# A fused four-layer graph network on one core: the first weight quarter loaded ahead of the activations, the first scale in halves, the first weight product read by VectorE, and three quarters of the second product computed later

## The chip, the core and the metric

One program on one core of a Trainium2 chip. The metric is the device time of the program in microseconds (us), median of several runs; lower is better. The engines are TensorE (PE for matmuls, PEld for the loading of their stationary side), VectorE (DVE), ScalarE (ACT), GpSimd (POOL) and the queue of SyncE (SP, or SPq), which issues most of the DMAs.

## The reference, cut to what matters

Four layers over 128 graphs of 64 nodes with 512 features (8192 rows in all). Each layer starts with a layer norm without weights and a relu, and adds its result to x. The first two are the ones whose setup the change touches:

```python
# layer 0
h = relu(layernorm(x))
q, k = split(h @ Wqk); v = h @ Wv
w = mask * sum(q * (adj @ (k * mask))) / sqrt(512)      # one number per row
x = x + softmax(w, axis=1)[:, :, None] * v
# layer 1
h = relu(layernorm(x))
weight = adj * exp((h @ Wq.T + bq) @ (h @ Wk.T + bk).T)
x = x + (weight / weight.sum(2)) @ (h @ Wv.T + bv)
```

Layers 2 (eight-head attention) and 3 (three-hop diffusion) follow. The kernel never forms q and k in layers 0 and 1: it multiplies the two weight matrices once, M0 = Wq Wk^T of layer 0 (called m0) and A1 of layer 1 (called a1), and then needs h M0 h^T.

## The kernel before, in words

The 8192 rows are cut into 16 groups (NG) of 512, each of four tiles of 128 rows. Every engine has one program, written out by hand in the order in which it runs; semaphores tie them together. There is no scheduler. The groups run through layers 0 and 1 together: iteration g does layer 0 of group g and layer 1 of group g-1.

A product of full precision goes over the array in fp32r as three passes: hi by hi, hi by lo and lo by hi (`gemm_T`, L309, and `gemm`, L330; both of 48 matmuls a group and matrix). So each matrix is split into `hi` (a rounding copy, usually on ACT, `split_W` L977) and `lo` (source minus hi, on DVE, `split_W` L598, or on POOL).

The setup, in the order of each engine:

- SP issues (L1474 on): x of group 0 (1024 KB); four quarters k = 0..3 of layer 0's Wqk, each as a qT and a kTw part of 256 KB; three small loads (two biases in `bcol`, the node mask in `mcol`; semaphore d_b1 counts all three); wk1 (1024 KB). Then `gather(0, 0, (0, 1))` waits until DVE has made the four transposes of group 0 (v_tr) and issues 8 DMAs of 64 KB that finish the transposition of h (hs to hGA). Behind the gather stand wq1 (1024 KB), adj and mask of group 0, Wv of layer 0, Wv of layer 1 (1024 KB each), bv1, bqk, then x of group 1, adj of group 1, mask of group 1 and x of group 2.
- PE (L371 on): m0, 16 full fp32 matmuls in the order k outside, output quarter dc inside, so that all four PSUM banks are finished in the last round; `s0`, a small matmul; `rows1`, eight matmuls, four with wk1 and four with wq1; `product("a1", wk1, wq1, (0, 1))`, two of the four output quarters of a1 (4 fp32 matmuls each). Then iteration 0: `l01_g0` (g0 = M0 by h, four banks oc 0..3), tile 0 of `l01_v0`, the scores s0 (`scores`, L334), tiles 1..3 of v0, then the other two quarters of a1, crow and ucol. `l01_g0` waits for p_flo0 (lo of h) and for v_wlo (lo of m0). The scores wait for a_g0, that is, for ACT's copies of all four g0 banks.
- DVE (L703 on): statistics of x0 (`stats_A`), bsel and bprod from bcol (wait for d_b1), four transposes into hs, the four lo parts of m0, the lo parts of h (`features0_lo`), s0, the two rows, lo of a1's quarters 0 and 1; then in iteration 0 statistics of x1, and `transposes(0, 1)`.
- POOL: `scale_A(0, 0)` (L1236) turns the statistics of four tiles into scale and offset by four small instructions, once all four tiles' statistics are there; then the mask product and the lo part of Wv0.
- ACT (L1046 on): `norm_A(0, 0)` (four tiles), then 8 gather DMAs of its own (q = 2, 3), then the four hi copies of m0, the hi copies of h (`features2_hi`), hi of Wv0, hi of a1's quarters 0, 1. Iteration 0: copies of g0's banks 0 and 1, then `norm_A(0, 1)` (needs x1 and its statistics), then copies of g0's banks 2 and 3.

Two places carry much of what follows. On ACT the four norms of x1 stand between two pairs of g0's copies (three lines of the loop, put together here for g = 0):

```python
g0(g, (0, 1))      # L1057
norm_A(0, 1)       # L1067
g0(g, (2, 3))      # L1069
```

and on PE the scores need all four copies (L423). `hi_of` and `lo_dve` (L292, L293) are only the counts that the semaphores of hi and lo parts reach, in the order of the names.

Of the kernel before, what the change touches and what calls it, by code (L numbers as in the profile page):

```python
# [66 lines left out]
def rows(w):  # L67
    return w.rearrange("(c p) n -> p c n", p=128)
# [6 lines left out]
def build(nc, x, adj_rows, adj_cols, adj_heads, nodemask, L0_gnn_Wqk, L0_gnn_Wv, L1_gnn_Wq_w, L1_gnn_Wq_b, L1_gnn_Wk_w, L1_gnn_Wk_b,  # L75
# [11 lines left out]
    with root:  # L87
# [3 lines left out]
        def sems(names):  # L91
            return [sem(n) for n in names.split()]
# [24 lines left out]


        (c_pool, a_whi, v_wlo, p_wlo) = sems("consts_pool w_hi w_lo_dve w_lo_pool")
        (v_bsel, v_rows1, v_crow, v_ucol, p_one1) = sems("bias_cols rows1 crow ucol ones_v")  # L120
        (v_af, v_cst, p_bones, p_bsum) = sems("af cst bones bsum")

# [166 lines left out]

        hi_of = {n: 4 * i + 4 for i, n in enumerate(("m0", "v0", "a1", "v1", "q2", "k2", "v2", "o2", "w2", "w1", "w0"))}  # L292
        lo_dve = {n: 4 * i + 4 for i, n in enumerate(("m0", "a1", "v1", "q2", "k2", "v2", "o2"))}  # L293
        lo_pool = {n: 4 * i + 4 for i, n in enumerate(("v0", "w2", "w1", "w0"))}

# [1 line left out]
        def pe_program(eng):  # L297
# [85 lines left out]
            for j, (w, loaded, c0) in enumerate(((wk1, d_k1, 0), (wq1, d_q1, 4))):  # L383
# [3 lines left out]
                    ins = eng.matmul(b[32 * k:32 * k + 32, :], bsel[:, c0 + k, :], w[:, k, :], start=True, stop=True,  # L387
                                     tile_position=(0, 32 * k))
                ins.then_inc(full, 1)
            product("a1", wk1, wq1, (0, 1))  # L390

            def l01_g0(g, ocs):
                pe.wait_ge(p_flo0, 4 * g + 4)
# [18 lines left out]
            for g in range(NG + 1):  # L412
                on0, on1, on_pv = g < NG, g >= 1, g >= 2
                if on0:
                    l01_g0(g, (0, 1))
                if on_pv:
                    l01_pv(g - 2)
                if g == NG:
                    l2_gemm_T("q2", 0, Wq2, a_q)
                if on0:  # L420
                    l01_g0(g, (2, 3))
                    l01_v0(g, 0)
                    pe.wait_ge(a_g0, 4 * g + 4)  # L423
                    scores(("s0", g), gT[0], hGA, (v_am, g + 1))
                    for t in range(1, 4):
                        l01_v0(g, t)
                if on1:
                    pe.wait_ge(p_flo1, 4 * g)
                    pe.wait_ge(v_wlo, lo_dve["a1"])
                    for oc in range(4):  # L430
                        gemm_T(("g1", g - 1, oc), Wa1, hT[1], oc, (a_g1, 4 * (g - 1) + oc + 1))
                    l01_v1(g - 1, 0)
                    pe.wait_ge(a_g1, 4 * g)
                    scores(("s1", g - 1), gT[1], hGB, (a_ex, 4 * g))
                    for t in range(1, 4):
                        l01_v1(g - 1, t)
                else:
                    product("a1", wk1, wq1, (2, 3))
                    b, full, before = bank.take(("crow",), (v_crow, 1))
                    pe.wait_ge(*before)  # L440
                    pe.wait_ge(v_rows1, 3)
                    eng.matmul(b[:], ones1[:], crow1[:], start=True, stop=True).then_inc(full, 1)
                    b, full, before = bank.take(("ucol",), (v_ucol, 1))
                    pe.wait_ge(*before)
                    for d in range(4):
                        ins = eng.matmul(b[:, d:d + 1], urow[:, d * 128:(d + 1) * 128], ones1[:, 0:1], start=True, stop=True)
                    ins.then_inc(full, 1)
# [118 lines left out]
            for g in range(NG):  # L566
                i = g % 2
# [24 lines left out]
        def dve_program(eng):  # L592
# [113 lines left out]
            eng.tensor_copy(bsel[:, :, 0], bcol[:]).then_inc(v_bsel, 1)  # L706
            eng.tensor_tensor(bprod[:], bcol[:, 0:4], bcol[:, 4:8], ALU.mult).then_inc(v_bsel, 1)
            transposes(0, 0)
            split_W(Wm0, "m0")
            features0_lo()  # L710
            dve.wait_ge(*bank.done(("s0",)))
            eng.tensor_reduce(s0, bank.of(("s0",))[:, 0:4], AX, ALU.add).then_inc(v_rows1, 1)
            for j, row in enumerate((crow1, urow)):
                dve.wait_ge(*bank.done(("rows1", j)))
                eng.tensor_copy(row[:], bank.of(("rows1", j))[:]).then_inc(v_rows1, 1)
            split_W(Wa1, "a1", (0, 1))

            for g in range(NG + 1):
                on0, on1, on_pv = g < NG, g >= 1, g >= 2
                if on_pv:  # L720
                    l01_x2(g - 2)
                if g + 1 < NG:
                    stats_A(0, g + 1)
                    if g == 0:
                        transposes(0, 1)
                elif on0:
                    stats_A(2, 0)
                if on0:
                    dve.wait_ge(*bank.done(("s0", g)))
                    dve.wait_ge(p_am, g + 1)  # L730
                    eng.tensor_tensor(am[:], t4(bank.of(("s0", g))[:, 0:256]), am[:], ALU.mult).then_inc(v_am, 1)
                    dve.wait_ge(v_am, g + 1)
                    dve.wait_ge(c_pool, 6)
                    eng.tensor_reduce(wS, am[:], AX, ALU.add).then_inc(v_amr, 1)
                    dve.wait_ge(v_amr, g + 1)
                    dve.wait_ge(d_b1, 48)
                    eng.scalar_tensor_tensor(wS, wS, ISQ, mcol[:, 4 * g:4 * g + 4], ALU.mult, ALU.mult).then_inc(v_ws, 1)
                    l01_p(g)
                    if g >= 2:
                        transposes(*((0, g + 1) if g + 1 < NG else (2, 0)))  # L740
                    xt = xs[x_slot(kA(0, g))]
                    for t in range(4):
                        dve.wait_ge(*bank.done(("v0", g, t)))
                        dve.wait_ge(v_pcol, g + 1)
                        eng.scalar_tensor_tensor(xt[:, t, :], bank.of(("v0", g, t))[:], pcol[:, t:t + 1], xt[:, t, :],
                                                 ALU.mult, ALU.add).then_inc(v_x1, 1)
                        dve.wait_ge(v_x1, 4 * g + t + 1)
                        stats(stB, v_stB, a_nB, 4 * g + t, xt, t)
                    if g == 1:
                        transposes(0, 2)  # L750
                    if g == 0:
                        split_W(Wa1, "a1", (2, 3))
                        split_in_place(Wv1, "v1")
                    transposes(1, g)
                    if on1:
                        l01_dots(g)
                    if g == NG - 1:
                        split_in_place(Wq2, "q2")
                        features2_lo(0)
                else:  # L760
                    stats_A(2, 1)
                    transposes(2, 1)
                    split_in_place(Wk2, "k2")
                if on1:
                    for t in range(4):
                        dve.wait_ge(*bank.done(("v1", g - 1, t)))
                        dve.wait_ge(d_bv1, 16)
                        if g >= 2:
                            dve.wait_ge(*bank.done(("pvy", g - 2, 1)))
                        b3, bias3 = (v[:].rearrange("p (c n) -> p c n", c=2) for v in (bank.of(("v1", g - 1, t)), bv1))  # L770
                        eng.tensor_tensor(vf[:, t, :, 0:256], b3, bias3, ALU.add).then_inc(v_vf, 1)
                else:
                    dve.wait_ge(*bank.done(("crow",)))
                    eng.tensor_copy(crow[:], bank.of(("crow",))[:]).then_inc(v_crow, 1)
                    dve.wait_ge(*bank.done(("ucol",)))
                    eng.tensor_copy(ucol, bank.of(("ucol",))[:, 0:4]).then_inc(v_ucol, 1)
                    l01_dots(0)
# [193 lines left out]
        def act_program(eng):  # L971
# [71 lines left out]
                    act.wait_ge(*bank.done((n, g, m)))  # L1043
                    eng.activation(dst[:, m, :], bank.of((n, g, m))[:], ACT.Identity, bias=bqk[:, c0 + m:c0 + m + 1]).then_inc(done, 1)  # L1044

            norm_A(0, 0)  # L1046
            act.wait_ge(v_tr, 4)
            blocks(eng, hGA, (2, 3))
            split_W(Wm0, "m0")
            features2_hi(0, 0, hT[0])  # L1050
            split_in_place(Wv0, d_v0)
            split_W(Wa1, "a1", (0, 1))

            for g in range(NG + 1):
                on0, on1 = g < NG, g >= 1
# [12 lines left out]
                if on0:  # L1068
# [15 lines left out]
                    else:  # L1084
                        features2_hi(2, 0, hT2[0])
                    if g == 0:
                        split_W(Wa1, "a1", (2, 3))
                        split_in_place(Wv1, d_v1)
                        norm_B(0, range(4))
                if on1:  # L1090
# [127 lines left out]
        def pool_program(eng):  # L1218
# [17 lines left out]
            def scale_A(layer, g):  # L1236
                scale(stA, v_stA, p_stA, 4 * kA(layer, g) + 4, 0, 4)
# [21 lines left out]
            eng.memset(wz[:], 0.0).then_inc(c_pool, 1)  # L1259
            eng.memset(stB[:, :, 11], 0.0).then_inc(c_pool, 1)  # L1260
            pool.wait_ge(s_pool, mh)
            scale_A(0, 0)
            l01_am(0)
            split_in_place(Wv0, "v0")
            for g in range(NG + 1):
# [105 lines left out]
        def sp_program(eng):  # L1371
# [99 lines left out]


            qk_rows = rows(L0_gnn_Wqk)
            load_x(0, x_v[0])  # L1474
            for k in range(4):
                eng.dma_start(qT[:, k, :], qk_rows[:, k, :]).then_inc(d_qk[k], 16)
                eng.dma_start(kTw[:, k, :], qk_rows[:, 4 + k, :]).then_inc(d_qk[k], 16)
            eng.dma_start(bcol[:, 0:4], L1_gnn_Wq_b).then_inc(d_b1, 16)
            eng.dma_start(bcol[:, 4:8], L1_gnn_Wk_b).then_inc(d_b1, 16)
            eng.dma_start(mcol[:], nodemask_cols).then_inc(d_b1, 16)  # L1480
            eng.dma_start(wk1[:], rows(L1_gnn_Wk_w)).then_inc(d_k1, 16)
            gather(0, 0, (0, 1))
            eng.dma_start(wq1[:], rows(L1_gnn_Wq_w)).then_inc(d_q1, 16)
            load_adj(0)
            load_mask(0)
            eng.dma_start(Wv0["raw"][:], rows(L0_gnn_Wv)).then_inc(d_v0, 16)
# [175 lines left out]
```

## Time and profile before

| | |
|---|---|
| median of 3 runs | 2223.53 us (2223.47 to 2223.89) |
| the profiled execution: its own time | 2223.11 us |
| its span (first to last instruction) | 2221.3 us |
| PE busy | 2203.8 us (99%) |
| PEld / DVE / ACT / POOL busy | 1759.2 / 1356.5 / 776.6 / 740.4 us |
| share of PE in the chain that ended last | 97% |
| granted TensorE clock over the span | 1.000 |
| DMA over the span | 99 GB/s |

Busy times overlap, since the engines run side by side; a busy PE isn't PE at its peak. The chain that ended last is followed back from the last instruction to what released each step. What the change touches lies in the first 70 us of the span, so the 40 slices of the page (55 us each) say little about it and the trace is read there in order of time.

### The profile page before, as it was taken

The page shows a single profiled execution, that of the slowest core. Times are in us where ns is not written, and L with a number is a line of the kernel's source. Part 1 is how long each engine was busy: PE and PEld are TensorE (multiplying, and loading weights), DVE is VectorE, ACT ScalarE, POOL GpSimd, SP SyncE. Part 2 cuts the span into 40 slices and gives each one's busy share as a digit, 9 for nine tenths or more (in the row PEclk, how much of TensorE's full clock was granted, in tenths as well). Part 3 has the DMA queues.
Part 4 walks back from the last instruction along what each step waited for, and adds up shares of the span by engine and source line. Part 5 has one row for each costly group of instructions (what it writes and reads, how often), then busy time and mean ns, then how long its engine had stood idle before and what let it go on. Part 6 is the DMA issues. An engine that isn't in the chain of part 4 may idle for free.

```text
span 2221.3 us, 39182 instructions
## 1 busy us (share of the span) xinstructions
PE 2203.8 (99%) x15756; PEld 1759.2 (79%) x15756; DVE 1356.5 (61%) x2712; ACT 776.6 (35%) x1393; POOL 740.4 (33%) x926
## 2 busy tenths in 40 slices
PE   8999999999999999999999999999999999999999
PEld 5788888888888888888888888888877777777776
DVE  4575666666665676555655454555687575757542
ACT  3433333233323333333322333232444343434342
POOL 1443433343433423332322332332343131313130
PEclk9999999999999999999999999999999999999999
DMA  6333332333333344433233323333443323233321
GB/s 211 77 80 101 96 103 84 86 95 89 87 92 94 102 136 126 114 86 94 83 101 100 106 82 95 88 97 92 144 151 112 105 87 103 88 100 92 95 60 38
DMA packets 142006, 220.52 MB, mean 99 GB/s; under 512 B 33920, under 2 KB 40064, under 8 KB 141824
## 3 DMA queue, kind: packets, MB, share of 16 engines
q1 hardware_dynamic: 135680, 209.62, 32.5%
q10 hardware_dynamic: 6144, 8.40, 1.6%
q8 instruction: 123, 2.02, 0.4%
q14 instruction: 59, 0.48, 0.1%
HBM read 84.71 MB, written 50.37 MB: 61 GB/s over the span
## 4 chain that ended last, share of the span: by engine, by line
PE 97%; DVE 2%; DMA 1%; issue 0%; SPq 0%; POOL 0%; ACT 0%; DVEq 0%; ACTq 0%; POOLq 0%
PE bank L326 54%; PE bank L316 32%; PE bank L342 3%; PE bank L559 3%; PE bank L496 1%; PE bank L466 1%; PE bank L363 1%; PE bank L306 1%; DVE yt L946 1%; PE bank L545 0%; DMA wq<-in_L_gnn_Wq_w 0%; DMA x<-in_x 0%; DVE hs L636 0%; DVE stA L611 0%; SPq L968 0%
## 5 line engine op out<-in xcount | busy, mean ns | idle before, releaser
L326 PE MATMUL bank<-w_hi,h3T_hi 128*128 128x512 f32 x768 | 305.6, 398 | 0.0
L326 PE MATMUL bank<-w_lo,h3T_hi 128*128 128x512 f32 x768 | 299.4, 390 | 0.0
L326 PE MATMUL bank<-w_hi,h3T_lo 128*128 128x512 f32 x768 | 299.1, 389 | 0.0
L975 ACT ACTIVATE Z<-bank 64x512 f32<-64x512 f32 x256 | 151.8, 593 | 320.5 <-PE bank L326 246.9
L326 PEld LDWEIGHTS bank<-w_hi,h3T_hi 128*128 128x128 f32 x768 | 144.1, 188 | 55.1 <-issue 26.0
L989 ACT ACTIVATE hn<-x,stA 128x512 f32<-128x512 f32 x192 | 141.6, 825 | 106.9 <-POOL stA L1234 106.9
L326 PEld LDWEIGHTS bank<-w_hi,h3T_lo 128*128 128x128 f32 x768 | 144.2, 188 | 30.4
L326 PEld LDWEIGHTS bank<-w_lo,h3T_hi 128*128 128x128 f32 x768 | 144.2, 188 | 28.9
L636 DVE STREAM_TRANSPOSE hs<-hn 128x512 f32<-128x512 f32 x192 | 124.2, 690 | 38.7 <-ACT hn L989 38.7
L931 DVE TENSOR_TENSOR yt<-bank,bsumt 128x512 f32<-128x512 f32 x64 | 43.9, 685 | 164.2 <-PE bank L559 164.2
L1044 ACT ACTIVATE QQ<-bank,bqk 128x512 f32<-128x512 f32 x64 | 43.9, 689 | 283.5 <-PE bank L316 276.5
L1242 POOL TENSOR_TENSOR h1T_lo<-hGB,h1T_hi 128x512 fp32r<-128x512 f32 x64 | 80.7, 1290 | 160.7 <-ACT h1T_hi L975 160.7
L611 DVE BATCH_NORM_STATS2 stA<-x 128x6 f32<-128x512 f32 x192 | 127.6, 664 | 8.5 <-DMA x<-in_x 8.0
L946 DVE SCALAR_TENSOR_TENSOR junk<-hn,arowt 128x512 f32<-128x512 f32 x112 | 132.7, 1244 | 0.0
L1312 POOL TENSOR_TENSOR x<-x,blk 128x512 f32<-128x512 f32 x64 | 82.5, 1322 | 126.7 <-ACT hn L989 122.0
L1229 POOL TENSOR_SCALAR stA<-stA 128x4 f32<-128x4 f32 x48 | 12.7, 264 | 331.5 <-DVE stA L613 331.4
L596 DVE TENSOR_TENSOR cT_lo<-bank,cT_hi 128x256 fp32r<-128x256 f32 x128 | 44.1, 416 | 127.5 <-ACT cT_hi L975 127.5
L1242 POOL TENSOR_TENSOR h0T_lo<-hGA,h0T_hi 128x512 fp32r<-128x512 f32 x60 | 90.4, 1536 | 92.4 <-ACT h0T_hi L975 92.4
L975 ACT ACTIVATE g0T<-bank 128x512 f32<-128x512 f32 x64 | 38.0, 597 | 233.2 <-PE bank L316 233.2
L1300 POOL TENSOR_TENSOR zt<-zt,sm 128x512 f32<-128x512 f32 x64 | 66.8, 1044 | 142.8 <-DVE sm L805 142.4
L1348 POOL TENSOR_TENSOR Town<-alt,rst 128x256 f32<-128x256 f32 x16 | 11.9, 742 | 306.2 <-DVE rst L913 306.2
L801 DVE TENSOR_TENSOR zt<-bank,adj 128x512 f32<-128x512 f32 x64 | 43.3, 676 | 110.9 <-PE bank L466 110.8
(201 smaller groups left out, 5853.3 us busy)
## 6 DMA issues: line engine op xcount, KB each, us to landing
hGA<-hs SPq DMA_DIRECT2D x760, 64.0 KB, 2.0
mid<-x SPq DMA_DIRECT2D x32, 1024.0 KB, 4.3
x<-mid SPq DMA_DIRECT2D x32, 1024.0 KB, 5.7
x<-in_x SPq DMA_DIRECT2D x16, 1024.0 KB, 5.8
hGB<-hs SPq DMA_DIRECT2D x256, 64.0 KB, 2.0
out<-x SPq DMA_DIRECT2D x15, 1024.0 KB, 4.6
PT<-hs SPq DMA_DIRECT2D x120, 64.0 KB, 2.0
PT<-hs ACTq DMA_DIRECT2D x120, 64.0 KB, 2.1
```

The costliest lines, as they stand in the source:

```text
L316: ins = eng.matmul(b[:], W[l][:, k, os], h[r][:, k, :], start=(k == 0 and i == 0), stop=(k == 3 and i == 2))
L326: ins = eng.matmul(b[:], h[l][:, k, ts], W[r][:, k, :], start=(k == 0 and i == 0), stop=(last and k == 3 and i == 2))
L342: ins = eng.matmul(b[h, t * 64:(t + 1) * 64], left[:, k, ts], right[:, 2 * i:2 * i + 2, 4 * k + t, :], start=(k == 0), stop=(k == 3))
L559: ins = eng.matmul(b[HALF[c], :], left, Z[zi][h, 2 * r + c, :], start=False, stop=True)
L611: m = dve.step(eng.bn_stats(st[:, t, 0:6], xt[:, t, :]))
L636: eng.transpose(hs[:, :, :, t, :].rearrange("p b c r -> p c b r"), (hn1 if layer == 1 else hn)[t][:].rearrange("p (c b r) -> p c b r", c=4 ...
L946: eng.scalar_tensor_tensor(unused, hn[t][:], 0.0, arow[:, c, :], ALU.max, ALU.mult, accum_out=scol[g % 2][:, t, c:c + 1]).then_inc(v_dotA, 1)
L975: return eng.activation(dst, src, ACT.Copy)
L989: eng.activation(h[t][:], xt[:, t, :], ACT.Relu, bias=st[:, t, 10:11], scale=st[:, t, 9:10]).then_inc(done, 1)
L1242: eng.tensor_tensor(by_token(h["lo"], q), hG[:, q], by_token(h["hi"], q).bitcast(F), ALU.subtract).then_inc(done, 1)
L1300: eng.tensor_tensor(z3, z3, s8(sm[r][:, 0:8]), ALU.subtract).then_inc(p_sb, 1)
L1312: eng.tensor_tensor(xt[:, t, :], xt[:, t, :], bo2, ALU.add).then_inc(p_xb, 1)
```

## The change

Five edits.

1. SP: the first quarter of Wqk (qT and kTw of k = 0) is issued ahead of x0; the other three quarters stay behind x0.
2. SP: wq1 is issued right behind wk1, ahead of the gather of group 0, no longer behind it.
3. POOL: the first scale runs as two halves, tiles 0, 1 after two tiles' statistics (semaphore p_st0) and tiles 2, 3 after four; ACT's norms of tiles 0 and 1 wait for the first half only.
4. m0: DVE makes the hi copy from the bank itself and then the lo part; ACT has no m0 work any more (so the counts of `hi_of` lose m0).
5. a1: only quarter 0 is computed ahead of iteration 0; quarters 1, 2 and 3 come behind tile 3 of v0 in iteration 0, with their splits on ACT and DVE.

```diff
-        hi_of = {n: 4 * i + 4 for i, n in enumerate(("m0", "v0", "a1", "v1", "q2", "k2", "v2", "o2", "w2", "w1", "w0"))}
+        hi_of = {n: 4 * i + 4 for i, n in enumerate(("v0", "a1", "v1", "q2", "k2", "v2", "o2", "w2", "w1", "w0"))}
 # PE
-            product("a1", wk1, wq1, (0, 1))
+            product("a1", wk1, wq1, (0,))
-                    product("a1", wk1, wq1, (2, 3))
+                    product("a1", wk1, wq1, (1, 2, 3))
 # DVE
-            split_W(Wm0, "m0")
+            for cc in range(4):
+                b = bank.of(("wT", "m0", cc))
+                dve.wait_ge(*bank.done(("wT", "m0", cc)))
+                eng.tensor_copy(Wm0["hi"][:, cc, :], b[:]).then_inc(v_mhi, 1)
+                dve.wait_ge(v_mhi, cc + 1)
+                lo_split(Wm0["lo"][:, cc, :], b[:], Wm0["hi"][:, cc, :]).then_inc(v_wlo, 1)
-            split_W(Wa1, "a1", (0, 1))
+            split_W(Wa1, "a1", (0,))
-                        split_W(Wa1, "a1", (2, 3))
+                        split_W(Wa1, "a1", (1, 2, 3))
 # ACT
-            norm_A(0, 0)
+            for t in range(4):
+                norm(hn, stA, p_stA if t > 1 else p_st0, 1, a_nA, xs[0], t)
             act.wait_ge(v_tr, 4)
             blocks(eng, hGA, (2, 3))
-            split_W(Wm0, "m0")
             features2_hi(0, 0, hT[0])
             split_in_place(Wv0, d_v0)
-            split_W(Wa1, "a1", (0, 1))
+            split_W(Wa1, "a1", (0,))
-                        split_W(Wa1, "a1", (2, 3))
+                        split_W(Wa1, "a1", (1, 2, 3))
 # POOL
-            scale_A(0, 0)
+            scale(stA, v_stA, p_st0, 2, 0, 2)
+            scale(stA, v_stA, p_stA, 4, 2, 4)
 # SP
-            load_x(0, x_v[0])
             for k in range(4):
                 eng.dma_start(qT[:, k, :], qk_rows[:, k, :]).then_inc(d_qk[k], 16)
                 eng.dma_start(kTw[:, k, :], qk_rows[:, 4 + k, :]).then_inc(d_qk[k], 16)
+                if k == 0:
+                    load_x(0, x_v[0])
...
             eng.dma_start(wk1[:], rows(L1_gnn_Wk_w)).then_inc(d_k1, 16)
+            eng.dma_start(wq1[:], rows(L1_gnn_Wq_w)).then_inc(d_q1, 16)
             gather(0, 0, (0, 1))
-            eng.dma_start(wq1[:], rows(L1_gnn_Wq_w)).then_inc(d_q1, 16)
```

## Rows read from the trace of the kernel before

**Rows 1.** Waits of PE over the whole span: total us, times, longest.

```profile
PE bank L376 <- DMA kTw<-in_L_gnn_Wqk: 7.8, 1, 7.8
PE bank L363 <- DVE vf L771: 1.8, 2, 0.9
PE bank L387 <- DMA wq<-in_L_gnn_Wq_w: 1.7, 1, 1.7
PE bank L559 <- ACT Tother L975: 0.9, 1, 0.9
```

**Rows 2.** Timeline of PE and PEld: start us, duration us, what, idle before.

```profile
7.82 15.79 PE L376 MATMUL bank<-kTw,qTw 128*128 128x512 f32 x32 [7.82 <-DMA kTw<-in_L_gnn_Wqk]
...
10.52 0.34 PEld L376 LDWEIGHTS bank<-kTw,qTw 128*128 128x128 f32 x1 [0.52 <-issue]
...
12.29 0.19 PEld L376 LDWEIGHTS bank<-kTw,qTw 128*128 128x128 f32 x1 [0.24 <-issue]
...
33.99 0.80 PE L316 MATMUL bank<-h0T_hi,m_hi 128*128 128x512 f32 x1
```

**Rows 3.** Timeline: x of group 1, g0's last two copies, the scores.

```profile
37.68 0.69 DVE L611 BATCH_NORM_STATS2 stA<-x 128x6 f32<-128x512 f32 x1 [1.69 <-DMA x<-in_x]
...
45.90 1.05 ACT L975 ACTIVATE g0T<-bank 128x512 f32<-128x512 f32 x2
...
48.12 2.08 PE L342 MATMUL bank<-hGA,g0T 128*64 128x64 f32 x64
```

**Rows 4.** Timeline of SP's DMA issues: start us, us for the issue.

```profile
0.72 0.44 SPq L1377 DMA_DIRECT2D x<-in_x  x1
...
15.52 5.04 SPq L968 DMA_DIRECT2D hGA<-hs  x8
20.60 0.58 SPq L1483 DMA_DIRECT2D wq<-in_L_gnn_Wq_w  x1
...
23.24 0.61 SPq L1486 DMA_DIRECT2D v_raw<-in_L_gnn_Wv  x1
...
26.55 0.57 SPq L1377 DMA_DIRECT2D x<-in_x  x1
27.17 2.39 SPq L1383 DMA_DIRECT2D abf<-in_adj_rows  x1
```

**Rows 5.** Landings: first users of x0, biases and Wv0, and the chain's row of wq1.

```profile
6.35 0.69 DVE L611 BATCH_NORM_STATS2 stA<-x 128x6 f32<-128x512 f32 x1 [6.35 <-DMA x<-in_x]
...
12.36 0.18 DVE L706 COPY bsel<-bcol 128x8 f32<-128x8 f32 x1 [2.72 <-DMA mcolt<-in_nodemask_cols]
...
31.06 2.19 ACT L975 ACTIVATE v_hi<-v_raw 128x512 fp32r<-128x512 f32 x4 [4.74 <-DMA v_raw<-in_L_gnn_Wv]
...
20.60 5.79 DMA wq<-in_L_gnn_Wq_w
```

**Rows 6.** Timeline of the path from x0 to h's lo part.

```profile
9.82 0.24 POOL L1229 TENSOR_SCALAR stA<-stA 128x4 f32<-128x4 f32 x1 [7.76 <-DVE stA L613]
...
11.81 2.93 ACT L989 ACTIVATE hn<-x,stA 128x512 f32<-128x512 f32 x4 [9.81 <-POOL stA L1234]
...
12.66 2.83 DVE L636 STREAM_TRANSPOSE hs<-hn 128x512 f32<-128x512 f32 x4
...
21.77 0.69 DVE L596 TENSOR_TENSOR m_lo<-bank,m_hi 128x512 fp32r<-128x512 f32 x1 [6.29 <-ACT m_hi L975]
...
24.96 2.49 DVE L596 TENSOR_TENSOR h0T_lo<-hGA,h0T_hi 128x512 fp32r<-128x512 f32 x4
```

**Rows 7.** Stretches: PE, PEld, DVE, ACT, POOL busy; clock, DMA share, GB/s last.

```profile
16.20:22.60 6.40, 6.40 (x17) 2.81 (x16) 0.69 (x1) 1.20 (x2) 0.00 (x0) 1.00 0.73 176
...
31.06:37.68 6.62, 6.62 (x24) 4.13 (x23) 1.39 (x3) 3.60 (x7) 5.00 (x4) 1.00 1.08 351
```

**Rows 8.** Timeline: lo part of group 1's h, and PE's first matmul with it.

```profile
63.24 1.27 POOL L1242 TENSOR_TENSOR h0T_lo<-hGA,h0T_hi 128x512 fp32r<-128x512 f32 x1 [0.17 <-ACT h0T_hi L975]
...
66.97 0.48 PE L316 MATMUL bank<-h0T_hi,m_hi 128*128 128x512 f32 x1
```

More of the change, by code:

```diff
@@ L119, in build @@
         (c_pool, a_whi, v_wlo, p_wlo) = sems("consts_pool w_hi w_lo_dve w_lo_pool")
+        p_st0, v_mhi = sems("scaleA_first m0_hi")
         (v_bsel, v_rows1, v_crow, v_ucol, p_one1) = sems("bias_cols rows1 crow ucol ones_v")
```

## The prediction

> **What bounds the kernel now.** I read the waits of PE first, because the table of the profile puts PE at 99% busy: all that can be won is time in which PE stands still, or matmuls that disappear, and this change removes no matmul. PE waits 12.2 us in all [rows 1]. 7.8 us of it is the start, until the first quarter of Wqk has landed; 1.7 us is wq1, in the setup; the other 2.7 us are hundreds of us later and nothing here touches them. So the change can give back part of 9.5 us at most, and only if no new wait of PE appears.
>
> Next I read the timeline of PE [rows 2]. m0 starts at 7.82, and its 32 array records (two for each fp32 matmul) first follow each other at 0.34 + 0.52 = 0.86 us, later at 0.19 + 0.24 = 0.43 us. A quarter of a1 is 8 such records, 3.43 us. g0 begins at 33.99 and the scores at 48.12 [rows 3], 14.13 us later, with no wait in between.
>
> Then the timeline of the other engines around these scores, because ACT copies g0's banks 2 and 3 only behind the norms of x1. x1 lands at 37.68 and the last copy ends at 45.90 + 1.05 = 46.95 [rows 3]: 9.27 us from landing to copy (statistics, scale, four norms, two copies). PE arrives at the scores at 48.12, so this chain has 1.1 us of slack. That number decides the case: whatever brings PE to the scores earlier than x1's chain comes back as a wait there.
>
> **The change part by part.**
>
> *First quarter ahead of x0.* x0 (1024 KB) landed 5.6 us after its issue, and the 512 KB behind it 1.47 us later, at 7.82 [rows 2, 4, 5]; that is 0.35 MB/us. With the quarter first, and both parts issued by 1.7 us, it lands at about 6.35 - 1.47 = 4.9, or a little later for the second issue: 5.0 (bounds 4.5 and 5.6). x0 then lands where the quarter did, at about 7.8. PE starts 2.8 us earlier. The other quarters come where they came before (the bytes ahead of them are the same), some 1.5 us apart behind 7.8, while PE needs about 5 us for the first quarter and 3.43 us for each other: no wait. m0 ends at about 5.0 + 15.4 = 20.4.
>
> *wq1 ahead of the gather.* Before it was issued at 20.60 and took 5.79 us [rows 4, 5]. Now it is issued near 8 us, follows wk1 and is there by 18 to 19; PE needs it at about 21.7. The wait of 1.7 us goes. SP saves 0.6 us of issue behind the gather.
>
> *Later x0, scale in halves.* Before: scale begins at 9.82, norms at 11.81, transposes at 12.66 [rows 6]. DVE's transposes also stand behind the copy of the biases at 12.36 [rows 5], and these land behind the same bytes as before. Statistics of two tiles take 1.6 us, so with x0 at 7.8 the first half of the scale begins at 9.4. It has the same four instructions on half the columns; bounds 1.5 and 2.0 us (2.0 is 9.82 to 11.81), I take 1.7. Norms 0 and 1 run from 11.1, norms 2 and 3 from about 12.9 to 14.4. The transposes, 0.71 us each, start at 12.66 as before and end at 15.5 as before. So x0's 1.45 us are hidden, by the wait for the biases and by the halves; without the halves hn0 would come at 14.1 and the gathers 1.4 us later. Slip of the gathers: 0 to 0.7 us, I take 0.1.
>
> *m0's parts on DVE.* ACT loses four copies that it could have begun only after its 8 gather DMAs, at about 20.9. The copy on DVE has no row; the subtraction from the same bank, 0.69 us [rows 6], is the nearest. So a pair is 1.35 to 1.5 us and four pairs 5.4 to 6.0. They begin when bank 0 is full, 2.6 us before m0's end, at 18.2 after the 0.43 us rhythm is counted back from the end, and end at 23.6 to 24.2. The lo parts of h, 2.49 us [rows 6], follow on DVE: g0 may start at 26.1 to 26.7. PE gets there at 20.4 + 0.4 (s0) + 2.0 (rows) + 3.43 (one quarter of a1) = 26.2. I take 26.3, a wait of 0.1. wq1 now shares the DMA engines with the gathers, which used them at 0.73 and moved 176 GB/s [rows 7], against a free stretch of 2 us ahead of them; the gathers may land up to 0.5 us later, which lies under DVE's m0 work.
>
> *One quarter of a1 less ahead, one more behind.* 3.43 us of PE move from before g0 to after v0. By itself this is zero: PE's total is the same. What it does is bring g0, and the scores, 3.43 us earlier than they would be.
>
> *The sum up to the scores.* g0 at 26.3 puts PE at the scores at 26.3 + 14.13 = 40.4. v0's lo part is no hindrance: Wv0 lands 31.06 - 23.24 = 7.8 us after its issue now, and even at 31.06 [rows 5] POOL's four subtractions would be done at 36.9, before 37.6.
>
> *Where x1 lands now.* x1's issue stays behind the gather [rows 4] and can come only 0.6 us earlier, at 25.9. In the old trace the stretch ahead of its landing is full (share 1.08, 351 GB/s [rows 7]), so the 1024 KB of wq1 taken out of the line are worth 1.05 MB / 0.351 = 3.0 us, less what the engines now stand idle until Wv0's data can start. Second count: Wv0, issued at 22.6, can't be there before 22.6 + 5.8 = 28.4 (wq1's time alone [rows 5]), and x1 followed Wv0 by 37.68 - 31.06 = 6.6 us: 35.0. First count with 0.6 us of idle time: 35.3. I take 35.1, bounds 34.2 (wq1's full 3.0 and half of the saved issue) and 35.9. Then the last copy of g0 ends at 35.1 + 9.27 + 0.1 = 44.5. The scores start there and not at 40.4: PE waits about 4.1 us.
>
> *From the scores on.* Before, 48.12; now 44.5 with one quarter of a1 (3.43 us) still owed: 44.5 - 48.12 + 3.43 = -0.2 us. Behind the scores the chain of group 1's h (gather after the scores, hi, lo) ends at 64.51 and PE wants it at 66.97 [rows 8]: 2.5 us of slack, which grows by the quarter of a1 that now stands in front. ACT's and DVE's work on a1 and v1 ends at the same distance from g0 of group 1 as before. So no further term. The three edits' 2.8 + 1.7 us reach PE, and about 4.1 us go again at the scores. The profiled span of 2221.3 becomes 2221.1, its own time of 2223.1 (1.8 us around the span, and 0.4 us below the median of the runs) 2222.9; at the median, 2223.53 - 0.2 = 2223.3 us.
>
> **A wait of 4 us and the clock.** The granted clock reads 1.00 in every stretch, but m0's first records followed each other at 0.86 us for some 4 us after 7.8 us of standing still: that is half speed, the 1.2 GHz level; the 0.43 us after that is 2.4 GHz [rows 2]. After the 1.7 us wait for wq1 there is no such stretch. A wait of 4.1 us lies between. The price, if the clock falls, is what it was at the start: half of 4 us, less one record, 1.7 us. I count zero, since 4.1 is nearer to 1.7 than to 7.8, and keep 1.7 for the range. The Trainium skill (TensorE: Matmul & The Clock Gate, section "Part 1: The HAM clock gate") says that an array left idle falls back to its half clock and gets full speed back only after sustained work, and it speaks against this change: by it the new wait would cost PE its speed, and the sum would be +1.5 instead of -0.2. The trace so far shows the half speed at the start, 0.86 against 0.43 us, and nothing on a wait of this length.
>
> **The rivals.**
>
> *PE is fed (0.10).* If x1 landed by 31.1, the scores would start at 40.4 and nothing be given back: 40.4 - 48.12 + 3.43 = -4.3 us, 2219.2. For it: 3.0 us of bytes leave the line. Against it: from 37.68 it would take 6.6 us, and x1 would land only 5.2 us after an issue at 25.9 with 2.3 MB ahead of it.
>
> *The clock falls in the wait at the scores (0.20).* The matmuls of the scores and the first of v0 run at half speed: -0.2 + 1.7 = +1.5 us, 2225.0. It decides from a wait somewhere between 1.7 and 7.8 us. This is the one that ends slower.
>
> *SP's queue backs up (0.10).* With more than 2 MB outstanding an issue took 2.39 us instead of 0.5 (the load of adj at 27.17) [rows 4]. If wq1's bytes do the same to the gather's issues, all that is behind them, x1 too, slips by up to 1.9 us: +1.7, 2225.2. It decides from a slip of 0.2 us. Against it: 7 us lie between wq1's issue and the gather.
>
> *The first quarter is not earlier (0.05).* If DMAs of 256 KB shared the engines with x0, PE would start at 7 rather than 5, arrive at the scores at 42.4, and still wait: the time stays 2223.3. The first edit is worth nothing by my account, whatever it does at the start.
>
> **How the numbers follow.** The forecast (0.50, with the last rival 0.55) is 2223.3, its own range 2222.3 to 2224.2, from x1's bounds (-0.9, +0.8). PE fed: 0.10. Clock or queue: 0.30, up to 2225.4. The remaining 0.05 is unnamed. The range 2221.2 to 2225.6 leaves out PE fed and the unnamed. A measurement of this kernel tells about 0.2% from no change, that is 4.4 us: even PE fed, at 4.3 us, stays just inside. Faster 0.03, same 0.94, slower 0.03 (a slip of x1 by over 4.6 us, or clock and queue together).
>
> **What the profile after would show.** Right: PE's first matmul near 5.0; no wait for wq1; g0 near 26.3; x1's statistics at 34 to 36; a new wait of PE for ACT's g0T, of 3 to 5 us, ahead of the scores near 44.5; g0 of group 1 at 66.8. Wrong in its main step: scores near 40.4 with no wait. Pairs of records 0.86 us apart behind the scores would show the clock; a late x1 with a late issue, the queue.

## The result and the profile after

The changed kernel takes 2228.07 us (median of 13 runs, 2226.79 to 2229.93), the kernel before 2223.09 us (13 runs, 2222.71 to 2223.89): ratio 1.0021, 95% interval 1.0014 to 1.0029. It is 5.0 us slower, just beyond the 4.4 us that I had named as what can be told from no change. The forecast was 2223.3, with a range that ended at 2225.6. The profiled execution took 2228.09 us, and its span is 2226.3, against 2221.3 before.

The waits of PE after (us in total, times, the longest), against [rows 1]:

```profile
PE bank L343 <- ACT g0T L981: 6.1, 1, 6.1
PE bank L377 <- DMA kTw<-in_L_gnn_Wqk: 4.2, 1, 4.2
PE bank L364 <- DVE vf L777: 1.8, 2, 0.9
PE bank L560 <- ACT Tother L981: 0.9, 1, 0.9
PE bank L327 <- issue: 0.4, 1, 0.4
PE bank L317 <- DVE h0T_lo L597: 0.2, 1, 0.2
```

The start cost 7.8 us and costs 4.2; the 1.7 us for wq1 are gone; a wait of 6.1 us for ACT's copies of g0 is new. The waits add up to 13.6 us against 12.2, so only 1.4 of the 5.0 us are in this table. The timeline of PE after, against [rows 2] and [rows 3]:

```profile
4.25 16.88 PE L377 MATMUL bank<-kTw,qTw 128*128 128x512 f32 x32 [4.25 <-DMA kTw<-in_L_gnn_Wqk]
...
22.05 1.04 PE L388 MATMUL bank<-wq,bsel 128*32 128x512 f32 x8
23.02 3.70 PE L307 MATMUL bank<-wq,wk 128*128 128x512 f32 x8
26.95 0.50 PE L317 MATMUL bank<-h0T_hi,m_hi 128*128 128x512 f32 x1 [0.23 <-DVE h0T_lo L597]
...
47.00 3.68 PE L343 MATMUL bank<-hGA,g0T 128*64 128x64 f32 x64 [6.13 <-ACT g0T L981]
```

g0 starts at 26.95 instead of 33.99, 7.0 us earlier (3.4 of it is the quarter of a1 that moved). PE reaches the scores at 40.87, stands until 47.00, and then the same 64 matmuls take 3.68 us instead of 2.08. The windows of both kernels say why; first the one after (busy us and count of PE, PEld, DVE, ACT, POOL, then granted clock, DMA share, GB/s):

```profile
22.00:26.00 4.00, 4.00 (x19) 1.57 (x12) 3.96 (x7) 2.14 (x4) 0.39 (x1) 1.00 0.68 123
26.00:37.67 11.67, 11.44 (x49) 8.88 (x48) 2.86 (x5) 3.88 (x7) 5.40 (x5) 1.00 1.00 330
...
44.00:47.00 3.00, 0.00 (x0) 0.00 (x1) 2.73 (x4) 2.95 (x5) 0.00 (x0) 0.54 0.00 0
47.00:50.00 3.00, 3.00 (x56) 3.00 (x58) 0.00 (x0) 0.00 (x0) 0.00 (x0) 0.50 0.00 0
50.00:53.00 3.00, 3.00 (x24) 2.52 (x21) 2.03 (x8) 0.00 (x0) 0.00 (x0) 0.82 0.20 46
```

The granted clock falls to 0.50, the 1.2 GHz level, while PE waits, and stays there until some 4 us behind the wait. The Trainium skill (TensorE: Matmul & The Clock Gate, section "Part 1: The HAM clock gate") says that an idle array drops to its half clock and gets full speed back only after work. The trace agrees.

The same view of the kernel before, for the transfers:

```profile
22.00:26.00 4.00, 2.73 (x14) 0.92 (x12) 3.50 (x6) 3.48 (x7) 0.00 (x0) 1.00 0.92 305
26.00:37.68 11.68, 11.25 (x39) 6.01 (x40) 4.10 (x9) 3.92 (x8) 5.72 (x5) 1.00 1.03 345
```

From 22 to 26 us the kernel before moved 305 GB/s x 4 us = 1.22 MB, the one after 0.49 MB. Of wq1's 1.05 MB that no longer stand there, 0.73 MB were not replaced: behind the gather the DMA engines are busy for 0.68 of the time instead of 0.92, and move less while they are busy. Another 0.18 MB are missing up to x1's landing (345 x 11.68 against 330 x 11.67). So x1 lands at 37.67, where it landed before. The timelines of DVE, ACT and SP after, against [rows 3 to 5]:

```profile
8.86 0.69 DVE L612 BATCH_NORM_STATS2 stA<-x 128x6 f32<-128x512 f32 x1 [8.86 <-DMA x<-in_x]
...
13.59 0.17 DVE L707 COPY bsel<-bcol 128x8 f32<-128x8 f32 x1 [1.43 <-DMA mcolt<-in_nodemask_cols]
...
23.88 3.01 DVE L597 TENSOR_TENSOR h0T_lo<-hGA,h0T_hi 128x512 fp32r<-128x512 f32 x4
...
37.67 0.69 DVE L612 BATCH_NORM_STATS2 stA<-x 128x6 f32<-128x512 f32 x1 [4.78 <-DMA x<-in_x]
```

```profile
29.28 2.20 ACT L981 ACTIVATE v_hi<-v_raw 128x512 fp32r<-128x512 f32 x4 [4.74 <-DMA v_raw<-in_L_gnn_Wv]
...
43.06 2.93 ACT L995 ACTIVATE hn<-x,stA 128x512 f32<-128x512 f32 x4 [9.72 <-POOL stA L1240]
45.89 1.05 ACT L981 ACTIVATE g0T<-bank 128x512 f32<-128x512 f32 x2
```

```profile
8.15 0.76 SPq L1490 DMA_DIRECT2D wq<-in_L_gnn_Wq_w  x1
16.41 5.04 SPq L974 DMA_DIRECT2D hGA<-hs  x8
...
23.56 0.61 SPq L1494 DMA_DIRECT2D v_raw<-in_L_gnn_Wv  x1
...
26.61 0.46 SPq L1384 DMA_DIRECT2D x<-in_x  x1
```

The last two copies of g0 stand on ACT behind 9.72 us of idle time and four norms of x1; g0's last matmul starts at 37.76, so their inputs were full soon behind 38 us.

**The 5.0 us in terms.** Scores 47.00 against 48.12: -1.1. The quarter of a1 still owed: +3.4. The half clock from the scores on: +1.8 (g0 of group 1 starts at 71.20, 24.20 behind the scores; before it was 67.10 - 48.12 = 18.98, and 3.43 more with the quarter, 22.41). That makes +4.1 at the start of group 1's g0, seen in the chain that ended last, first after, then before (it counts the scores before from 48.19, 0.07 behind their first record):

```profile
47.00 3.68 PE bank L343 x64
...
71.20 11.02 PE bank L317 x48
```

```profile
48.19 2.02 PE bank L342 x64
...
67.10 11.02 PE bank L316 x48
```

The offset stays at 4.1 through two layers. The last 0.9 us come at 860, at the start of layer 2, which no edit touches:

```profile
859.60 6.80 DVE L597 TENSOR_TENSOR v2w_lo<-v2w_raw,v2w_hi 128x512 fp32r<-128x512 f32 x4
```

The same four subtractions took 5.77 us before. All run while POOL makes a row of adds; the longest of them takes 1.78 us, and a subtraction of the same size takes 0.68 with POOL idle (k2w_lo, just ahead of them in the trace after). Before, the first of the four began at 855.52, between two of POOL's adds, and took 0.68; after, the shortest took 1.72. In the profiled executions of all kernels here the term was 0.1 us or less in the seven where the shortest took under 1.1 us, and between 0.05 and 0.9 in the others. No run tested it, so that POOL's adds cause it is not shown.

### The profile page after: what moved, and what is told of

It is laid out like the page before. It is cut to its first block, busy times and chain, and to the rows that moved or that the text cites. A ratio compares the mean times of both kernels' runs of the same rounds, so it can differ in the third digit from the quotient of the medians.

```text
span 2226.3 us, 39183 instructions
## 1 busy us (share of the span) xinstructions
PE 2207.1 (99%) x15756; PEld 1761.1 (79%) x15756; DVE 1360.0 (61%) x2716; ACT 774.8 (35%) x1389; POOL 742.6 (33%) x930
## 4 chain that ended last, share of the span: by engine, by line
PE 95%; DVE 2%; DMA 1%; SPq 1%; issue 0%; ACT 0%; POOL 0%; DVEq 0%; ACTq 0%; POOLq 0%
PE bank L327 54%; PE bank L317 31%; PE bank L343 3%; PE bank L560 3%; PE bank L497 1%; PE bank L467 1%; PE bank L364 1%; DVE yt L952 1%; DMA x<-in_x 0%; PE bank L307 0%; DVE v2w_lo L597 0%; PE bank L546 0%; DMA mcolt<-in_nodemask_cols 0%; DVE stA L612 0%; SPq L974 0%
## 5 line engine op out<-in xcount | busy, mean ns | idle before, releaser
L612 DVE BATCH_NORM_STATS2 stA<-x 128x6 f32<-128x512 f32 x192 | 127.4, 663 | 14.1 <-DMA x<-in_x 13.6
L1235 POOL TENSOR_SCALAR stA<-stA 128x4 f32<-128x4 f32 (+1 forms) x49 | 12.9, 262 | 334.0 <-DVE stA L614 333.9
```

What stands on the lines that cost most here:

```text
L612: m = dve.step(eng.bn_stats(st[:, t, 0:6], xt[:, t, :]))
```

## The experiments

All times are medians of ten runs, taken beside 25 to 31 runs of the kernel before on the same chip, and ratios are to that kernel (its medians were 2223.05 to 2223.28 us). Expectations stand as they were on record before each run.

**The order on ACT.** The changed kernel, with ACT's two last copies of g0 ahead of the norms of x1 in iteration 0 (norm_B and all else stay):

```
-                if g == 0:
-                    norm_A(0, 1)
                 if on0:
                     g0(g, (2, 3))
+                if g == 0:
+                    norm_A(0, 1)
+                if on0:
```

> The changed kernel, but in iteration 0 ACT copies all four banks of g0 ahead of the four norms of x1. Order theory (the loss is x1's chain standing ahead of g0's last two copies, and the clock that falls in that wait): no wait of PE at the scores, scores near 41 instead of 47.0 and 2.1 us long instead of 3.7, time 6.1 + 1.6 + 0.2 = 7.9 us below the changed kernel, near 2220, which is about 3 us below the kernel before. Rival (the wait only moves): group 1's h is late next, because its norms, transposes and gather hang on x1 too; then PE waits ahead of g0 of group 1 and less than 4 us come back.

2219.29 us (2218.84 to 2220.91), ratio 0.9983 [0.9974, 0.9993]. x1 even landed later here, at 39.18, and PE did not wait. Its waits of over 0.5 us and the scores:

```profile
PE bank L377 <- DMA kTw<-in_L_gnn_Wqk: 4.9, 2, 4.4
PE bank L364 <- DVE vf L777: 1.7, 2, 0.9
PE bank L560 <- ACT Tother L981: 0.9, 1, 0.9
```

```profile
40.91 2.08 PE L343 MATMUL bank<-hGA,g0T 128*64 128x64 f32 x64
```

Scores at 40.91, clock 1.00: 40.91 - 48.12 + 3.43 = -3.8. Two lines of order on ACT are worth 8.8 us of the changed kernel's time: 6.1 of wait, 1.8 of clock and the 0.9 at layer 2. The wait does not move on to a place further down.

**The same order in the kernel before**, the same diff, as a control:

> Control: the kernel before with ACT's four copies of g0 ahead of the norms of x1, none of the five edits. Order theory: PE came to the scores after the copies already (1.1 us of slack), so nothing changes: 2223.1, PE's waits 7.8 and 1.7 us as before. Rival (the new order of ACT is a gain by itself, and the five edits had little part in the 2219.3 of the run with copies first): near 2220.

2223.23 us, 0.9999 [0.9989, 1.0008]. There PE came to the scores later than the copies, by the 1.1 us that I had read; the order was free, and is the bound only once the other edits are in.

**x1 earlier.** The changed kernel, with x1 issued right behind Wv0:

```
+            load_x(1, x_v[1])
             eng.dma_start(Wv1["raw"][:], rows(L1_gnn_Wv_w)).then_inc(d_v1, 16)
...
-                    if g not in (2, 3):
+                    if g not in (1, 2, 3):
                         load_x(kA(0, g), x_v[g])
```

> The changed kernel, but x of group 1 is issued right behind Wv0, ahead of Wv1, bv1 and bqk. Order theory: x1 lands 3 to 4 us earlier (near 34), the last copy of g0 ends near 43, PE waits about 2.5 us and not 6.1, the clock stays at 1.00, time 3.5 + 1.6 = 5 us below the changed kernel, 2223. Rival (x1's landing is set by something other than its place in the line): it lands near 37 again and nothing changes.

2221.82 us (2221.17 to 2223.75), 0.9994 [0.9985, 1.0003], 1.2 us below what I expected. x1's statistics began at 32.48 without a wait, so it was there by then, and PE's wait shrank to 2.3 us. Yet the clock fell, against the expectation; it reads 1.00 over the wait and 0.64 over the 2.2 us behind it:

```profile
41.80 3.20 PE L343 MATMUL bank<-hGA,g0T 128*64 128x64 f32 x64 [2.33 <-ACT g0T L981]
```

**Edit 5 alone.** The kernel before, with one quarter of a1 moved behind v0 (product and both splits, as in the change):

```
-            product("a1", wk1, wq1, (0, 1))
+            product("a1", wk1, wq1, (0,))
...
-                    product("a1", wk1, wq1, (2, 3))
+                    product("a1", wk1, wq1, (1, 2, 3))
...
```

> The kernel before with the fifth edit alone: one quarter of a1 ahead of g0, three behind. Order theory: PE comes to the scores 3.43 us earlier (44.7), waits 2.3 us for copies that end at 46.95, and owes a quarter more: +2.3 us over the kernel before, near 2225.4, clock at 1.00. Rival (moving the quarter is free): no change, 2223.1.

2225.33 us (2224.29 to 2227.20), 1.0010 [1.0001, 1.0020].

```profile
46.92 2.08 PE L342 MATMUL bank<-hGA,g0T 128*64 128x64 f32 x64 [2.37 <-ACT g0T L975]
```

46.92 - 48.12 + 3.43 = +2.2: of 3.4 us that PE came earlier, 1.1 were slack and the rest a wait. Here 2.37 us of waiting did not lower the clock (64 matmuls in 2.08 us); in the run before this one 2.33 us did.

**Edit 5 undone**, with the order of the change (first) and with the copies first (second):

```
-            product("a1", wk1, wq1, (0,))
+            product("a1", wk1, wq1, (0, 1))
...
-                    product("a1", wk1, wq1, (1, 2, 3))
+                    product("a1", wk1, wq1, (2, 3))
...
```

> The changed kernel with its fifth edit undone: two quarters of a1 ahead of g0, two behind. Order theory: PE comes to the scores 3.43 us later (44.3), waits 2.7 us for the same copies and starts them at 47.0 as well; one quarter less is owed behind, so the time falls by 3.43, and by 1.6 more if a wait of 2.7 us leaves the clock alone: 5.0 us below the changed kernel, near 2223. If the clock falls in a wait of 2.7 us too: 3.4 below, 2224.6. Rival (the fifth edit is harmless and the start or the DMAs cost the time): no change.

2225.66 us (2224.06 to 2227.43), 1.0011 [1.0002, 1.0020]: 2.7 us above the 2223 that I expected with the clock up, and 1.1 above the 2224.6 with the clock down. In its profile x1 landed at 39.16, 1.5 us later than in the changed kernel, PE waited 4.1 us, and the clock fell again.

> The changed kernel with copies first and its fifth edit undone: two quarters of a1 ahead of g0. Theory: once the scores don't wait for x1, the place of the second quarter is worth only the 0 to 0.3 us that g0 waits for h: 2219.0 to 2219.3. Rival (the fifth edit brings something, since it lets the group's chain start 3.43 us earlier): 2220 or more.

2219.24 us (2218.49 to 2220.49), 0.9982 [0.9972, 0.9991]; scores at 43.37 without a wait, -4.8. Once PE is fed, edit 5 is worth nothing.

**The other edits, each undone with the copies first.** What each is worth is counted from the 2219.29 us of the first run, which was taken on another chip; the kernel before took 2223.14 us there and 2223.20 to 2223.28 beside these four.

Edit 1 (x0 ahead of the first quarter again):

```
+            load_x(0, x_v[0])
             for k in range(4):
...
-                if k == 0:
-                    load_x(0, x_v[0])
```

> The changed kernel with copies first (2219.3) and its first edit undone: x0 is issued ahead of all quarters again. Theory: PE starts at 7.8 and not 4.4, but at full rhythm from there, as m0's later quarters no longer come late; m0 ends at 23.4 instead of 21.5, the features are ready at about 26.5, so g0 starts 1.5 to 2.5 us later than 27.1 and the time is 2221 to 2222. Rival (the first quarter's start is eaten by x0 landing later and the gathers slipping): 2219.3 or less.

2222.30 us (2221.36 to 2225.16): edit 1 is worth 3.0 us.

Edit 2 (wq1 behind the gather again):

```
-            eng.dma_start(wq1[:], rows(L1_gnn_Wq_w)).then_inc(d_q1, 16)
             gather(0, 0, (0, 1))
+            eng.dma_start(wq1[:], rows(L1_gnn_Wq_w)).then_inc(d_q1, 16)
```

> The changed kernel with copies first and its second edit undone: wq1 behind the gather again. Theory: wq1 is issued near 21.5 and there near 27.3, PE needs it at 22.6 and waits 4 to 5 us, and the clock may fall in it (plus 1 to 2 us); 2223 to 2226. Rival (wq1's bytes slow the gathers as much as its early issue gives): 2220.

2227.11 us (2225.28 to 2228.16): worth 7.8 us, and 1.1 us above the range that I expected.

```profile
26.67 1.94 PE L388 MATMUL bank<-wq,bsel 128*32 128x512 f32 x8 [4.88 <-DMA wq<-in_L_gnn_Wq_w]
```

With m0 earlier, wq1 is late by 4.9 us instead of 1.7, and the granted clock is 0.50 from 25.9 to 32.6. x1 landed at 37.32: with a megabyte more behind the gather, 0.35 us earlier than without it.

Edit 3 (one scale of four tiles, norms behind it):

```
-            scale(stA, v_stA, p_st0, 2, 0, 2)
-            scale(stA, v_stA, p_stA, 4, 2, 4)
+            scale_A(0, 0)
...
-            for t in range(4):
-                norm(hn, stA, p_stA if t > 1 else p_st0, 1, a_nA, xs[0], t)
+            norm_A(0, 0)
```

> The changed kernel with copies first and its third edit undone: one scale over four tiles. Theory: in the run with halves the first norm begins 1.5 us behind the second tile's statistics; with the whole scale it begins 2.0 us behind the fourth's, 2.0 us later, hn0 is ready at about 16, transposes and gathers start 1.4 us later, and g0 waits for h's lo part: 2220.5 to 2221. Rival (the biases' landing sets the transposes anyway): 2219.3.

2220.35 us (2218.32 to 2221.51): 1.1 us, about as expected but within the spread of both.

Edit 4 (ACT copies m0's hi parts, behind its blocks of the gather; DVE has split_W in place of its four pairs):

```
             blocks(eng, hGA, (2, 3))
+            split_W(Wm0, "m0")
             features2_hi(0, 0, hT[0])
...
```

> The changed kernel with copies first and its fourth edit undone: ACT makes the hi copies of m0. Theory: ACT is held by its gather DMAs until 22.7; its four copies follow back to back by 0.55 us to 25, then four copies of h to 27.2, and DVE's last lo part comes near 28, so g0 waits about 1 us more: 2220 to 2220.5. Rival (DVE's pairs cost as much as ACT's lateness): 2219.3.

2221.24 us (2219.42 to 2222.05): 1.9 us, 0.7 more than expected, and the spreads overlap here too; g0 had to wait 1.6 us for h's lo parts.

**Why x1 did not come earlier.** First theory: x1 shares the engines with the loads issued behind it. SP waits for x1 before it issues them:

```
                         load_x(kA(0, g), x_v[g])
+                    if g == 1:
+                        sp.wait_ge(*x_loaded(1))
```

> The changed kernel, but SP waits for x1 to land before it issues adj and mask of group 1 and x of group 2. Interleaving theory (x1 came 8.4 us behind Wv0 instead of 6.6 because loads issued behind it took part of the engines): x1 lands at 36 to 36.5 instead of 37.7, and the time falls by 1.2 to 1.7, near 2226.5. Rival (the bytes ahead of x1 alone set it, and the line starts when Wv0's data start): x1 lands at 37.7, time 2228, at most moved by where x0 lands in the run.

2227.74 us (2226.40 to 2229.10), 1.0019 [1.0010, 1.0028]. x1 was issued at 27.65 and landed at 38.56, 10.9 us later, as before with company behind it. This theory fell.

The run shows something else. With nothing behind x1, the DMA share and rate ahead of its landing can be read (columns as in the windows above):

```profile
35.00:36.00 1.00, 1.00 (x7) 0.81 (x6) 0.00 (x0) 0.00 (x0) 1.00 (x2) 1.00 1.04 391
36.00:37.00 1.00, 1.00 (x6) 0.84 (x5) 0.00 (x0) 0.00 (x0) 0.27 (x1) 1.00 0.54 207
37.00:38.50 1.50, 1.50 (x9) 1.23 (x8) 0.00 (x0) 0.00 (x0) 0.00 (x0) 1.00 0.09 33
```

By 37.0 all but 0.05 MB (33 GB/s x 1.5 us) had moved, and that rest took 1.5 us more. The semaphore records of the trace say the same: each load signals sixteen landings, one for each part of it, and only the last lets its user start. x1's came from 36.26 to 38.53. In the kernel before, Wv0's came from 29.41 to 29.81 with one straggler at 31.04, and x1's from 35.66 to 36.73 with one at 37.66; in the changed kernel they came from 28.87 to 29.26, and from 35.28 to 37.65. From first part to first part x1 is 6.3 us behind Wv0 before and 6.4 after. So of the step from 6.6 to 8.4 us, 1.2 us is the straggler of Wv0 that the old trace had and the new one has not.

Second theory: SP's place. The first adj and mask loads go ahead of the gather, so that Wv0 and x1 stand right behind it:

```
-            gather(0, 0, (0, 1))
             load_adj(0)
             load_mask(0)
+            gather(0, 0, (0, 1))
```

> The changed kernel, but adj and mask of group 0 are issued ahead of the gather, in SP's idle time, and no longer between gather and Wv0. Theory (wq1's bytes left the line, but their place was empty: in the changed kernel the DMA engines moved only 94 GB/s between 24 and 26, small mask pieces and nothing else, until Wv0's data came): Wv0 and x1 are issued 2.0 us earlier, Wv0 lands near 27.3, x1 near 35.5, PE's wait at the scores is about 4 us, time about 2226. Rival (x1's landing is bound by something else): x1 at 37.7, 2228.

2226.84 us (2225.60 to 2228.16), 1.0016 [1.0007, 1.0025], 1.2 us below the changed kernel where I expected 2. x1 was issued at 24.75 and landed at 36.42, 0.9 us later than I expected. The stretch from 22 to 26 us now moved 263 GB/s instead of 123, at a share of 1.00 instead of 0.68, so that gap was one of the order of issues; but x1 still followed Wv0 by 8.4 us.

Third, x0 ahead of the first quarter again (the diff of edit 1 above), so that the gathers come sooner, in the order of the change:

> The changed kernel with its first edit undone: x0 ahead of all quarters. Theory (the quarter ahead of x0 makes x0, the gathers and with them x1's issue later, and PE's earlier start only lengthens the wait at the scores): gathers near 15.0 instead of 16.4, x1 lands near 36.2, the last copy of g0 ends near 45.5, PE comes to the scores at 44.4 and waits 1.1 us with the clock up: 45.5 - 48.12 + 3.43 = +0.8 us over the kernel before, 2224, that is 4 us below the changed kernel. Rival (the first edit is neutral, since x1 sets the scores either way): 2228.

2225.63 us (2222.94 to 2226.16), 1.0010 [1.0001, 1.0019]: 1.6 us above what I expected, and still 2.4 us faster than the changed kernel, though PE starts 3.4 us later. x1 landed at 36.51, PE waited 2.8 us, and the clock fell. The same edit is worth +3.0 us with the copies first and costs 2.4 without.

Last, the two best together, edit 5 undone, copies first, and the masks ahead:

> The fastest version so far (changed kernel, copies first, two quarters of a1 ahead; 2219.2) with adj and mask of group 0 ahead of the gather. Theory: the scores don't wait for x1 there, so an earlier x1 brings nothing: 2219.2, or up to 0.5 more where the mask's pieces lie ahead of wq1 or of the gathers. Rival: 2218 or less.

2219.39 us (2218.57 to 2220.74), 0.9984 [0.9974, 0.9993]. x1 at 37.07 changes nothing when nobody waits for it. The three versions in which PE is fed at the scores and edits 1 to 4 stay can't be told apart: 3.7 to 4.0 us below the kernel before.

## Why the prediction was wrong

The mechanism was right: PE's time at the start is won and given back at the scores, behind x1 and ACT's order. The step that failed is **Where x1 lands now**, and with it the clock, which I counted at zero. By the profiles, -0.2 becomes -0.2 + 2.5 (scores at 47.0, not 44.5, since x1 landed at 37.67, not 35.1) + 1.8 (clock) + 0.9 (layer 2, a term that the sum did not have) = 5.0, as measured.

- *First quarter ahead of x0*: 5.0 predicted, 4.25 measured. x0 at 7.8 predicted, at 8.86 measured; in the runs with the quarter ahead it scattered from 8.1 to 10.3, with x0 first it lay between 6.2 and 6.4. Here too it is the last of sixteen parts: they came from 5.57 to 6.33 before, and from 6.83 to 8.84 after. PE's start gained 3.6 us and m0's end only 2.5 (20.96 instead of 23.45; 20.4 predicted). I had counted 5 us for the first quarter; all of it ran in the 0.86 us rhythm, and it took 6.0 (PEld after; the last load of weights at that rhythm, and the first of the second quarter):

```profile
9.50 0.34 PEld L377 LDWEIGHTS bank<-kTw,qTw 128*128 128x128 f32 x1 [0.52 <-issue]
10.23 0.19 PEld L377 LDWEIGHTS bank<-kTw,qTw 128*128 128x128 f32 x1 [0.39 <-DMA kTw<-in_L_gnn_Wqk]
```

  "No wait" for the other quarters was wrong as well: in six of the runs with the quarter ahead PE waited 0.5 to 2.0 us for the second one.
- *wq1 ahead of the gather*: right, no wait. Its byproduct was not: the 1.05 MB taken from behind the gather were to bring x1 3.0 us forward. I divided bytes by the rate of a full stretch, where the rate did not stay full: 0.73 MB of them were simply not moved in the four us before. I had allowed 0.6 us for that.
- *Scale in halves*: slip of the gathers 0.1 predicted (bound 0.7), 0.9 measured [rows 4], as x0 came 1.1 us later than counted and the biases at 13.59 instead of 12.36, ahead of DVE's transposes.
- *m0's parts on DVE*: a pair in 1.3 us, 1.35 to 1.5 predicted. g0 at 26.95, predicted 26.3: PE was there at 26.72 (26.2 predicted), 0.5 us late from m0, and the lo parts of h, 3.01 us instead of 2.49, held it 0.2 us more.
- *The sum up to the scores*: PE there at 40.87, predicted 40.4.
- *Where x1 lands now*: 35.1 predicted, 34.2 to 35.9 as bounds, 37.67 measured. In parts: issued at 26.61 instead of 25.9 (+0.7); Wv0 at 29.28, 5.7 us behind its issue as predicted but 0.9 late; x1 8.4 us behind Wv0 instead of the 6.6 that I carried over from the old trace (+1.8), 1.2 of which was Wv0's straggler there. x1's landing followed its issue by 11.0 us here and 11.1 before, and by 10.4 to 12.5 in every run where it kept its place. A second count by this figure, 25.9 + 11.1 = 37.0, was in the same rows, and I did not make it.
- *From the scores on*: 9.27 us from x1 to the last copy predicted, 46.94 - 37.67 = 9.27 measured. The chain of group 1 gave no further wait, as said.
- *The clock*: I gave it 0.20 and priced it 1.7; it cost 1.8. The wait was 6.1 rather than 4.1 us, but the runs show that 4.1 can suffice: it fell with waits of 2.3, 2.8, 4.0, 4.1, 4.9, 6.1 and 6.8 us, and stayed up with 1.7 [rows 1] and 2.4. "Nearer to 1.7 than to 7.8" was no ground for zero.
- *PE is fed*, priced at -4.3: what the first experiment does by another way, -3.8. I looked for it in an earlier x1, where the order of two lines on ACT decides.
- *SP's queue*: the gather's issues took 5.04 us as before [rows 4]. That rival fell where I had it; the queue did back up earlier, where one issue of the third quarter took 1.48 us (at 3.60).

Open: why the parts of x1, and of x0 behind the quarter, land up to 3.3 and 3.5 us apart (for x1 not from interference from behind, as the run with the held loads shows); why the clock fell with a wait of 2.3 us and not with one of 2.4; and the 0.9 us at layer 2.

## What to carry to other kernels

When work ahead of a meeting point gets faster, the gain is the slack of the latest other arrival and no more; look on each engine at what stands in program order between that arrival and what is needed, because reordering there (here two copies ahead of four norms) can be worth more than all edits upstream. Time a late load from its own issue in the queue that it will stand in, not by bytes removed ahead of it over a full stretch's rate: a queue that is fed by issues goes empty instead. Look at when the first and the last part of a load came before a distance between two landings is carried over. Price every new wait of TensorE of 2 us and more with the clock's fall: here it fell with seven of eight waits from 2.3 us on.

## What the runs showed of the hardware

- The granted clock fell with waits as short as 2.3 us (not with one of 2.4). With those of 2.3, 2.8 and 4.1 us it still reads 1.00 over the wait and falls behind it. A fall cost 1.5 to 2.6 us of PE's time from the scores on (with three quarters of a1 behind them, g0 of group 1 began 23.8 to 24.9 us later, against 22.3 with the clock up).
- x1's landing stayed 10.4 to 12.5 us behind its issue, with wq1's megabyte ahead of it or not (37.32 with, 37.67 without).
- A load of 1024 KB that shares the queue with 512 KB ahead of it landed anywhere from 8.1 to 10.3 us in profiled executions; with nothing ahead, 6.2 to 6.4. Its sixteen parts landed up to 3.5 us apart there (6.71 to 10.26 in the run with the whole scale), and 0.8 us apart with nothing ahead.
- A DVE subtraction of two 128x512 tensors took 0.68 us with POOL idle and up to 1.8 us while POOL was adding.
